# Modulation rows made in the last chunk by GpSimd, and z's first products moved: a state-space and feed-forward kernel on one core

## The reference

```python
mod = (silu(c) @ wmod).reshape(B, 6, 1, 256)
sa, ca, ga, sb, cb, gb = mod parts, one row of 256 per batch
ga = sign(ga) * max(abs(ga), 0.25)          # gb likewise, sign(0) = +1
h = layernorm(x) * (1 + ca) + sa
yf = sigmoid(mamba_f(h)); yb = sigmoid(mamba_b(h reversed in time)) reversed back
d = layernorm(0.5 * (yf + yb)) * ln_g + ln_b
x = x + ga * (d + h)
h = layernorm(x) * (1 + cb) + sb
h = silu(w1(h) * w1_s) * (w2(h) * w2_s)
h = gelu(h1(h) * h1_s); h = gelu(h2(h) * h2_s)
out = x + gb * (w3(h) * w3_s)
```

## Time and profile before

| what | value |
|---|---|
| median of three runs | 4865.73 us |
| the profiled execution | 4866.13 us |
| its span, first to last instruction | 4864.3 us |
| TensorE busy | 4310.0 us (89%) |
| VectorE busy | 4006.5 us (82%) |
| ScalarE busy | 3249.3 us (67%) |
| GpSimd busy | 3436.0 us (71%) |
| mean granted TensorE clock | 0.962 |

### The profile page before, as it was taken

How to read it: one execution, slowest core, us unless ns; L and a number is a source line. 1 busy time by engine, 2 the same in 40 slices (tenths; PEclk the granted TensorE clock), 3 DMA queues, 4 the chain that set the end, 5 groups by cost and what they waited for, 6 DMA issues and landing times. The chain is left out here.

```text
span 4864.3 us, 61578 instructions
## 1 busy us (share of the span) xinstructions
PE 4310.0 (89%) x22500; PEld 3152.6 (65%) x22500; DVE 4006.5 (82%) x4251; ACT 3249.3 (67%) x5210; POOL 3436.0 (71%) x1599
## 2 busy tenths in 40 slices
PE   8888888888888888888888888887689999999999
PEld 3555555566555556656555665565578888888888
DVE  6999999999999999999999999999844444445452
ACT  7777777777777777777777777777344444444443
POOL 5999999999999999999999999999600000000000
PEclk9999999999999999999999999999889999999999
DMA  7433333333333333333333333334130101010100
GB/s 262 139 124 121 118 113 113 116 115 121 116 112 117 121 111 122 114 114 109 118 114 109 112 113 120 111 108 152 57 117 31 35 31 35 31 35 31 32 25 9
DMA packets 176418, 474.96 MB, mean 98 GB/s; under 512 B 15024, under 2 KB 99376, under 8 KB 141488
## 3 DMA queue, kind: packets, MB, share of 16 engines
q1 hardware_dynamic: 175216, 459.44, 28.0%
q10 hardware_dynamic: 896, 11.54, 0.8%
HBM read 435.27 MB, written 47.19 MB: 99 GB/s over the span
## 5 line engine op out<-in xcount | busy, mean ns | idle before, releaser
L1244 DVE TENSOR_TENSOR_SCAN m_h<-bank,m_state,m_dBx 128x512 f32<-128x512 f32 x1792 | 2181.9, 1263 | 34.8 <-ACT bank L1033 29.1
L772 PEld LDWEIGHTS bank<-ident,m_h 128*128 128x128 f32 x8192 | 1010.3, 147 | 653.1 <-issue 332.7
L772 PE MATMUL bank<-ident,m_h 128*128 128x128 f32 x8192 | 1246.5, 284 | 165.6 <-DVE m_h L1253 104.4
L1140 POOL TENSOR_TENSOR m_dBx<-u,m_Bs 128x1024 f32<-128x1024 f32 x512 | 1202.8, 2388 | 3.1 <-DVE m_h L1276 1.2
L1140 POOL TENSOR_TENSOR m_dBx<-m_u,m_Bs 128x1024 f32<-128x1024 f32 x512 | 1200.5, 2377 | 2.1
L1253 DVE TENSOR_TENSOR m_h<-m_h,bank 128x1024 f32<-128x1024 f32 x736 | 880.4, 1196 | 27.7 <-PE bank L754 24.2
L1033 ACT ACTIVATE bank<-m_dt,cols 128x512 f32<-128x512 f32 x1024 | 691.4, 688 | 247.0 <-DVE m_h L1244 243.6
L1033 ACT ACTIVATE bank<-dt,cols 128x512 f32<-128x512 f32 x1024 | 690.4, 688 | 204.7 <-DVE m_h L1244 201.5
L754 PEld LDWEIGHTS bank<-ident,m_Ct 128*128 128x128 f32 x2944 | 346.5, 143 | 676.3 <-DVE m_h L1253 456.9
L754 PE MATMUL bank<-ident,m_Ct 128*128 128x128 f32 x2944 | 486.3, 290 | 315.0 <-DVE m_h L1253 312.6
L292 POOL TENSOR_TENSOR mvj<-mvj,norm_c 128x4 f32<-128x4 f32 x16 | 16.2, 1015 | 1058.3 <-DVE mvj L253 1058.3
(11 more groups left out here) (169 smaller groups left out, 5198.4 us busy)
## 6 DMA issues: line engine op xcount, KB each, us to landing
m_Bs<-b_dram SPq DMA_DIRECT2D x256, 1024.0 KB, 4.8
m_Cs<-c_dram SPq DMA_DIRECT2D x288, 256.0 KB, 3.2
xx<-in_x SPq DMA_DIRECT2D x16, 512.0 KB, 7.2
xn_dram<-xx SPq DMA_DIRECT2D x16, 512.0 KB, 4.4
yb_dram<-m_ysb SPq DMA_DIRECT2D x16, 512.0 KB, 6.8
xx<-xn_dram SPq DMA_DIRECT2D x16, 512.0 KB, 3.9
x_dram<-m_ysb SPq DMA_DIRECT2D x16, 512.0 KB, 6.8
base<-xn_dram SPq DMA_DIRECT2D x16, 512.0 KB, 3.9
```

The costliest lines, as they stand in the source:

```text
L772: mm = pe.matmul(YB[b][:, o:o + P], h[:, k % NH, m, tok:tok + P], ident[:, :], start=(s == 0 and o == 0), stop=False, is_transpose=True, s ...
L1140: pool.tensor_tensor(dBx[:, k % NDBX, :, :], u[ch.batch][:, m, :], Bs[:, k // BP % 2, k % BP, :].unsqueeze(1).broadcast_to((P, 2, T)), ALU ...
L1244: dve.tensor_tensor_scan(h[:, k % NH, m, flip(ch)], DA[ch.at(STEPS, i) % NDA][:, flip(ch)], dBx[:, k % NDBX, m, flip(ch)], initial, ALU.mu ...
```

## The change

1. **Rows in the last chunk.** TensorE makes the six row products and the columns of the second norm as seven jobs on bank 1, at steps AT_ROWS of the last chunk (in the place of `front`, which that chunk has not). ScalarE drains each, four steps after its start: rows straight into the tile `gain` (eight copies of 128x256), columns into `mod`, the added 1 as its bias.
2. **Factors by GpSimd.** The 21 steps are split into 13 (`branch`: what the join needs) and 8 (`ffn`: what the output needs), in place in `gain`. At the end of mamba GpSimd makes only `branch` of batch 0, and the three base steps of the first chunk. VectorE there joins (steps 0 and 1) ahead of the last two gates and goes on behind them. `branch` of batch 1 and both `ffn` are made by GpSimd at the start of the feed-forward block, with ln_g, ln_b and w3_s loaded again, into `ot`.
3. **In the first feed-forward chunk** VectorE makes chunk 1's base at the first tile of h1 (before: ahead of chunk 0), each step of join and norm stands one tile later, and two waits for the factors are added.
4. **The first preparation** has z's products at steps 33, 46, 38, 52, the last two roundings at 40 and 43 and the last two sums at 43 and 48.

```diff
 NFB = 2
+FIRST_Z = (33, 46, 38, 52)
+FIRST_START = {**START, **dict(zip(J_Z, FIRST_Z))}
+AT_ROWS = (16, 21, 26, 30, 32, 37, 41)
+R_MOD, R_BANK = 3, 1
...
-CAST_AT = (4, 7, 9, 13, 17, 22, 30, 35, 38, 43, 50)
-SUM_AT = (10, 10, 18, 18, 27, 28, 33, 36, 41, 46, 52)
+CAST_AT = (4, 7, 9, 13, 17, 22, 30, 35, 38, 40, 43)
+SUM_AT = (10, 10, 18, 18, 27, 28, 33, 36, 41, 43, 48)
...
-def make_gains(eng, S, sem, rows, q, lng, gain, sgn, mag, t):
...
+def gain_rows(gain, q, part):
+
+    return gain[:, {GA: 0, CA: 1, SA: 2, GB: 3}[part], q, :]
+
+
+class Gains:
...
+    BRANCH, FFN = 13, 8
...
+    def step(self, ins):
+        self.n += 1
+        ins.then_inc(self.S["gain_p"], 1)
+        self.pool.wait_ge(self.S["gain_p"], self.n)
...
+    def away_from_zero(self, g, sgn, mag, t):
+        pool = self.pool
+        self.step(pool.tensor_scalar(sgn, g, 0.0, None, ALU.is_ge))
+        self.step(pool.tensor_scalar(mag, g, 0.25, None, ALU.max))
+        self.step(pool.tensor_tensor(mag, mag, sgn, ALU.mult))
+        self.step(pool.tensor_scalar(sgn, g, 0.0, None, ALU.is_lt))
+        self.step(pool.tensor_scalar(t, g, -0.25, None, ALU.min))
+        self.step(pool.tensor_tensor(t, t, sgn, ALU.mult))
+        self.step(pool.tensor_tensor(g, mag, t, ALU.add))
+
+    def branch(self, q, gain, lng, sgn, mag, t):
+
+        pool = self.pool
+        ga, ca, sa = gain_rows(gain, q, GA), gain_rows(gain, q, CA), gain_rows(gain, q, SA)
+        self.away_from_zero(ga, sgn, mag, t)
+        self.step(pool.tensor_scalar(ca, ca, 1.0, None, ALU.add))
+        self.step(pool.tensor_tensor(ca, ga, ca, ALU.mult))
+        self.step(pool.tensor_tensor(sa, sa, lng[:, 1, :], ALU.add))
+        self.step(pool.tensor_tensor(sa, ga, sa, ALU.mult))
+        self.step(pool.tensor_scalar(ga, ga, 0.25, None, ALU.mult))
+        self.step(pool.tensor_tensor(ga, ga, lng[:, 0, :], ALU.mult))
...
+    def ffn(self, q, gain, lng, sgn, mag, t):
+
+        gb = gain_rows(gain, q, GB)
+        self.away_from_zero(gb, sgn, mag, t)
+        self.step(self.pool.tensor_tensor(gb, gb, lng[:, 2, :], ALU.mult))
...
-            def before(jobs):
-                return sum(BANK[k] == b and START[k] < START[i] for k in jobs)
+            def before(jobs, start=START):
+                return sum(BANK[k] == b and start[k] < start[i] for k in jobs)
...
-                return b, before(FRONT)
+                return b, before(FRONT, FIRST_START)
+            more = len(AT_ROWS) if b == R_BANK and (body == NALL or body == NALL - 1 and i in MID) else 0
...
-            return b, ch.at(nf + nm + nt, off - back * (nf + nm + nt))
+            return b, ch.at(nf + nm + nt, off - back * (nf + nm + nt) + more)
+
+        def row_job(e):
+
+            last = Chunk(NPASS - 1, NC - 1, 1)
+            return job(last, next(i for i in MID if BANK[i] == R_BANK))[1] - len(AT_ROWS) + e
...
-                    k = g - AT_Z[m]
+                    k = g - (FIRST_Z if ch.first() else AT_Z)[m]
                     if 0 <= k < KM:
                         part(ch, J_Z[m], k, KM, w_in[:, k, (KI + m) * P:(KI + m + 1) * P], hT[:, k, :])
...
@@ -803,6 +825,8 @@
                             turn_y(ch, g, m)
                         if has(ch, 1):
                             front(ch.go(1), g)
+                        else:
+                            rows(g)
...
-            def make_rows(b, j):
-                if b == 0 and j == 0:
-                    pe.wait_ge(S["wm2_in"], 16 * 6)
-                    pe.sem_inc(S["go"], 1)
-                    pe.wait_ge(S["scan"], STEPS * NALL)
-                if b == 1:
-                    pe.wait_ge(S["rows"], j + 1)
-                for k in range(KM):
-                    mm = pe.matmul(DA[j][:, :], cbc[:, k, b, :], wm(k, j), start=(k == 0), stop=(k == KM - 1))
-                mm.then_inc(S["rows_mm"], 1)
-
-            def rest_of_mod():
-                for j in range(6, 10):
-                    for k in range(KM):
-                        mm = pe.matmul(CB[:, 2 * j:2 * j + 2], wm(k, j // 4)[:, j % 4 * P:(j % 4 + 1) * P], cs[:, k, :],
-                                       start=(k == 0), stop=(k == KM - 1))
-                mm.then_inc(S["mod_mm"], 1)
+            def rows(g):
+
+                for e, at in enumerate(AT_ROWS):
+                    k = g - at
+                    if not 0 <= k < KM:
+                        continue
+                    bk = FB[R_BANK]
+                    if k == 0:
+                        if e == 0:
+                            pe.wait_ge(S["wm2_in"], 16 * 6)
+                            pe.sem_inc(S["go"], 1)
+                        pe.wait_ge(drain[R_BANK], row_job(e))
+                    if e == R_MOD:
+                        if k == 0:
+                            for j in range(6, 10):
+                                for i in range(KM):
+                                    mm = pe.matmul(bk[:, 2 * j:2 * j + 2], wm(i, j // 4)[:, j % 4 * P:(j % 4 + 1) * P],
+                                                   cs[:, i, :], start=(i == 0), stop=(i == KM - 1))
+                            mm.then_inc(fill[R_BANK], 1)
+                        continue
+                    b, j = divmod(e, R_MOD + 1)
+                    mm = pe.matmul(bk[:, :], cbc[:, k, b, :], wm(k, j), start=(k == 0), stop=(k == KM - 1))
+                    if k == KM - 1:
+                        mm.then_inc(fill[R_BANK], 1)
 
             def flush(ch):
                 for k in range(T_LAG):
@@ -854,14 +885,9 @@
                         spread_c(ch, NU + k - W_LAG)
                     for b in range(2):
                         turn_h(ch, NU + k - T_LAG, b)
-                    if 1 <= k <= 3:
-                        make_rows(0, k - 1)
                 turn_skip(ch, 1)
-                rest_of_mod()
                 for m in (2, 3):
                     turn_y(ch, AT_Y[m], m)
-                for j in range(3):
-                    make_rows(1, j)
                 for g in range(AT_Y[3] + 1, STEPS):
                     tail(ch, g)
 
...
-                    if g == AT_Z[m] + KM - 1:
+                    if g == (FIRST_Z if ch.first() else AT_Z)[m] + KM - 1:
                         wait_filled(act, ch, J_Z[m])
                         b = BANK[J_Z[m]]
                         act.copy(z[:, q, m, :], FB[b][:, :]).then_inc(drain[b], 1)
...
+            def rows(g):
+                for e, at in enumerate(AT_ROWS):
+                    if g != at + KM - 1 + ACT_LAG:
+                        continue
+                    act.wait_ge(fill[R_BANK], row_job(e) + 1)
+                    bk = FB[R_BANK]
+                    if e == R_MOD:
+                        for o, plus in ((6, 0.0), (8, 1.0)):
+                            ins = act.activation(mod[:, o:o + 2, :], bk[:, 2 * o:2 * o + 4].rearrange(
+                                "p (j b) -> p j b", b=BATCH), ACT.Identity, bias=plus)
+                    else:
+                        b, j = divmod(e, R_MOD + 1)
+                        for part in (2 * j, 2 * j + 1):
+                            if part in (SA, CA, GA, GB):
+                                o = part % 2 * DM
+                                ins = act.copy(gain_rows(gain, b, part), bk[:, o:o + DM])
+                    ins.then_inc(drain[R_BANK], 1)
...
                     if has(ch, 1):
                         front(ch.go(1), k)
                         xi_silu(ch.go(1), k)
+                    else:
+                        rows(k)
                     z_silu(ch, k)
...
                 evacuate(ch, 1)
                 for g in range(STEPS):
                     tail(ch, g)
-                for j in range(3):
-                    act.wait_ge(S["rows_mm"], 4 + j)
-                    act.copy(Bs[:, 0, j, :], DA[j][:, :]).then_inc(S["rows"], 1)
...
             def flush(ch):
                 for k in range(NU - W_LAG, NU):
                     weigh_c(ch, k)
+                pool.wait_ge(S["skip"], ch.at(KI, KI))
+                pool.sem_inc(S["go"], 1)
+                pool.wait_ge(S["lng_in"], 64)
+                pool.sem_inc(S["go"], 1)
+                pool.wait_ge(drain[R_BANK], row_job(len(AT_ROWS)))
+                Gains(pool, S, 0).branch(0, gain, lng, *(xi[:, i, 0:DM] for i in range(3)))
+                for step in range(3):
+                    J.make_base(pool, Chunk(0, 0, 0), step)
                 J.powers(pool, Chunk(0, 0, 0))
-                pool.wait_ge(S["rows"], 6)
-                make_gains(pool, S, "gain_p", rows(1), 1, lng, gain, xD[:, 0, 0:DM], xD[:, 1, 0:DM], xD[:, 2, 0:DM])
...
             def flush(ch):
                 for k in range(NU - W_LAG, NU):
                     weigh_c(ch, k)
-                for j in range(3):
-                    dve.wait_ge(S["rows_mm"], j + 1)
-                    dve.tensor_copy(xi[:, j, :], DA[j][:, :]).then_inc(S["rows"], 1)
-                dve.wait_ge(S["rows"], 3)
-                dve.sem_inc(S["go"], 1)
-                dve.wait_ge(S["lng_in"], 64)
```

(43 more changed lines are left out.)

35 lines of the change are left out of this document (5 added, 30 removed).

## The result

The changed kernel took 4838.45 us (median of 6 runs, 4835.43 to 4838.97), the kernel before 4866.05 in the same comparison: ratio 0.9942, 95% interval 0.9929 to 0.9955, so 27.6 us faster. The forecast was 32.4 us faster and 4833.7 us; the range held the time. The profiled execution took 4838.41 us (span 4836.5).

A forecast was written before the change was run, and what follows sets the result against it. GpSimd's line paces the state-space part, TensorE bounds the feed-forward part, one barrier joins them. Sum: -1.1 + 0.5 - 32.8 + 1.0 = -32.4, from 4866.1 to 4833.7 us; range 4828 to 4842.

The forecast's parts named there:

- the chain that was forecast: Joint: GpSimd's branch and base steps, last weighing, join 0, gates, then y's store; barrier ends at 3504.7 instead of 3537.47.
- Part 1, the first preparation: Moved z products let GpSimd's first m_dBx start at 69.5 against 70.60: -1.1 us, bounds -2.0 and +1.0.
- Part 2, the last chunk: Row products and ScalarE's copies added to the last chunk of the state-space part: +0.5 us, bounds 0 and +3.
- the job at step 32: Last chunk: two steps behind the job at 30, holds TensorE about 1 us, with the spreading of C queued behind.
- Part 3, the joint: End of state-space part up to the feed-forward part's first transpose: -32.8 us, bounds -38 and -29.
- The forecast gained 8.6: Joint: the last two gates done at 3495.4, before 3503.98, a gain of 8.6 us.
- from barrier to TensorE's first transpose 5.83 us, taken as unchanged: Start of feed-forward part: 5.83 us (3537.47 to 3543.30) stays; no gain from TensorE's clock, 3.5 us left to the range.
- My rival in which the feed-forward part starts faster: Behind the barrier: clock kept or code there sooner, 3.5 us gained, 4830.2 us; chance 0.07.
- Part 4, the feed-forward part: GpSimd's 29 steps beside VectorE's residues in the first feed-forward chunk: +1.0 us, bounds 0 and +5.
- the 4 us: First feed-forward chunk: if VectorE's residues and GpSimd's steps block each other fully, the sum is up to 4 us.
- the rule of the Trainium skill: VectorE instructions with two SBUF inputs and GpSimd instructions reading SBUF exclude each other; as lock rival 4838.7 us, chance 0.11.
- no row against a rule on two inputs: Joint: xn, four in 1.89 us beside GpSimd's 0.87 steps, cited against the lock rule, which wanted over 3 us.

The follow-up runs named there:

- run 8: Kernel before with only the move of z's products (with copies, casts, sums) in the first preparation: 4866.31 us, ratio 0.9999.
- run 5: Changed kernel with unused products put into TensorE's waits at the end of the state-space part: 4836.53 us, ratio 0.9938.
- run 9: Changed kernel with the feed-forward part's first transposes put ahead of the reading of the flag: 4831.71 us, ratio 0.9928.
- run 10: Changed kernel with the first transposes ahead of the flag and z's products back in their old places: 4832.17 us, ratio 0.9929.
- run 12: As run 9, with SyncE's three loads of weights held back until the first feed-forward job is filled: 4836.07 us, ratio 0.9934.
- run 1: Changed kernel with z's products, roundings and sums of the first preparation back at their old steps: 4834.47 us, ratio 0.9933.
- run 2: Changed kernel with all 29 remaining GpSimd factor steps back ahead of the barrier, behind its powers: 4854.27 us, ratio 0.9975.
- run 3: Changed kernel with SyncE's loads behind the barrier held back until TensorE's first transposes are done: 4836.79 us, ratio 0.9937.
- run 4: Changed kernel with only TensorE's one-pass program, flag neither read nor jumped on, so inputs needing several passes are left out: 4827.89 us, ratio 0.9921.
- run 7: Changed kernel once more, word for word: 4838.54 us median, ratio 0.9943; its profiled execution took 4832.74 us.
- run 11: As run 9, with the flag read early, in TensorE's last steps of the state-space part, into a register: 4828.96 us, ratio 0.9924.
- run 6: Changed kernel with row products of 2 columns in place of 512, so modulation rows are not computed: 4834.07 us in one run.

## Why the prediction was right, and where it was off

**Right: the direction, the size within 4.8 us, and the place.** The joint alone carries the gain, by the chain that was forecast, with no new wait of VectorE for GpSimd's base steps.

**Part 1, the first preparation.** The working held within 0.1 us at the first m_dBx (69.60, forecast 69.5). Over all profiles it starts at 69.16 in the mean of the eleven kernels with z's move (68.36 to 69.68) and at 70.40 in the three without. What failed is the last step, that -1.1 there is -1.1 at the end: 0.43 is left by 3410, and alone the move is worth 0.06 us (run 8), with an interval of 4 to 5 us to either side. VectorE's gates drift back over the chunks; by 3410 the profiles lie within some 5 us of one another, whatever the kernel, more than the step is worth. Which wait takes the gain back was not found.

**Part 2, the last chunk.** Forecast +0.5. It grew by 0.93 us where the clock fell around 3420 to 3425 (the changed kernel, runs 5, 9, 10, and 12 with 3425 to 3430) and by 0.31 where it stayed at 1.00 (runs 1, 2, 3, 4, 7, 11); with products of 2 columns by 0.0 (run 6). The size was right, by luck: the mechanism was another. The 0.5 was the job at step 32, which was to hold TensorE for about 1 us until its bank was drained; in the trace TensorE goes straight on from an output product (3432.65) to that job's (3433.52). What costs are the long products themselves, in front of the spreading of C that VectorE waits for.

**Part 3, the joint.** From last scan to the end of the gates, before 3503.98 - 3479.70 = 24.28; after 3496.44 - 3480.21 = 16.23; in run 7, with the clock up, 15.77. The forecast gained 8.6, run 7 gained 8.5. From there to the store 9.0 us in run 7, as before, and 10.65 in the changed kernel's first profile. The missing term is TensorE's clock ahead of the barrier: in the kernel before it had row products in every gap and 1.00 from 3480 to 3510; these are gone, and in 4 of the 11 profiles with the changed joint and no fillers the first output products take 5.38. I asked what the clock does behind the barrier and not what it does ahead of it. That removing the row products is the reason is argued, not shown: run 5 put work back and had the clock up, but so had seven of the eleven without it.

**The step that failed most: "from barrier to TensorE's first transpose 5.83 us, taken as unchanged".** It measured 7.67 by the same marks (end of the store's issue, 3507.46, to 3515.13), and the stretch is 7.2 to 7.6 in all five profiles with this joint and nothing changed behind it. The 5.8 was no fixed price: TensorE had been standing at the barrier for 25 us. Run 2 gives that back and has 5.47. Run 4 shows that all of it belongs to flag and jump, runs 9 and 11 split it: reading the flag 2.9, the jump at least 1.9. Run 3 shows that SyncE's loads make 2.1 of it, run 12 that these are not the weights'. So what was hidden in part behind a long wait came onto the path when the wait went. The DMA records place it (run 4): from the packet of the jump's code on it is 2.5 to 2.6 us before, in the changed kernel and in run 2, and the 1.8 us that came on top lie ahead of it, where the flag is read (4.67 in place of 2.87). Why that reading is shorter where TensorE has long stood at the barrier is not shown. My rival in which the feed-forward part starts faster had the sign wrong: it started later.

**Part 4, the feed-forward part.** Forecast +1.0, measured +0.3 to +0.4 (1321.4 against 1321.1 in run 2 and 1321.0 before; 1321.2 to 1321.5 in runs 1, 5, 6 and 7). The eight residues of the first stage took 0.68 to 1.20 us beside GpSimd in place of 0.68, 1.9 us more in all; but they have idle time between them, and only the last one's end counts. VectorE and GpSimd in order of time:
```profile
3531.54 0.74 POOL L325 TENSOR_TENSOR xn<-xn 128x256 f32<-128x256 f32 x1
3531.63 1.20 DVE L1620 TENSOR_TENSOR ga<-raw,ga 128x512 fp32r<-128x512 f32 x1
3532.37 1.17 POOL L326 TENSOR_SCALAR xn<-gain 128x256 f32<-128x256 f32 x1
...
3535.11 0.74 POOL L328 TENSOR_TENSOR xn<-xn 128x256 f32<-128x256 f32 x1
3535.25 1.14 DVE L1620 TENSOR_TENSOR ga<-raw,ga 128x512 fp32r<-128x512 f32 x1
```
Where a two-input step of GpSimd started first, it took its 0.74, and the residue ended 0.55 us behind that step's end: here twice (3532.83 after 3532.28, 3536.39 after 3535.84), and once more at 3537.07. Where the residue was under way first, GpSimd's step is the late one: 1.17 in place of 0.86 at 3532.37. So of two such instructions one waits for the other, whoever was first, and here the trace agrees with the rule of the Trainium skill on which the prediction drew (SBUF — State Buffer, Who interferes with whom). Behind a one-input step of GpSimd the residues lost less, 0.83 and 0.79. That all this did not cost the 4 us is due to the idle time between the residues. xn in the joint, four in 1.38 now, took 1.89 before and 1.88 in run 2 with GpSimd's small steps beside it, and before those steps kept their 0.87 and 0.85. It reads one tile, so it is no row against a rule on two inputs, as the prediction took it to be; it is slowed in part.

**The sum.** Against the profiled span: barrier 30.1 earlier in place of 33.4 (last scan 1.1 later than forecast, one weighing 0.5, output products 1.7), stretch +1.9 in place of 0, feed-forward 0.6 better: 3.3 + 1.9 - 0.6 = 4.6 of the 32.4.

Run 11 beats both kernels: 4828.96 us, 38.3 under the kernel before, and does all that they do. Run 4 is faster still by 1.1, within its scatter, and does less. What makes the clock fall ahead of the barrier in some executions stays open.
